# Self-attentions of a two-layer decoder: the product of the reciprocals at the head of TensorE's next turn, VectorE's normalisation behind the next tile's maxima and centred scores

## The chip, the core and the metric

The kernel runs on one core of a Trainium2 chip. The metric is the device time of one execution in microseconds. In the text PE is TensorE (PEld its weight loads), DVE is VectorE, ACT is ScalarE, POOL is GpSimd and SP is SyncE. L460 is line 460 of the kernel before.

## The reference, cut to what matters

`x` is (64, 64, 128) in float32: 64 sequences of 64 rows. Six blocks follow each other; the change is in the two self-attentions, which are the first block of each layer.

```python
x = x + L0_attn(layernorm(x))        # 16 heads of 8, biases, rotary embedding, causal
x = x + L0_xattn(layernorm(x), ctx, ctx, ...)
x = x + L0_ffn(layernorm(x), ...)
x = x + L1_attn(layernorm(x))        # 16 heads of 8, distance bias, causal
x = x + L1_xattn(ctx, layernorm(x), ...)
x = x + L1_ffn(layernorm(x), ...)

# inside an attention
scores = einsum('bhqd,bhkd->bhqk', q, k) / sqrt(8) + mask
attn = softmax(scores, axis=-1)
out = einsum('bhqk,bhkd->bhqd', attn, v).reshape(B, S, 128) @ wo
```

## The kernel before

The 4096 rows are cut into 32 tiles of 128 rows (two sequences each). `attention` is called for layer 0 (`rope` true) and layer 1. Each engine has a function `turn(t, u)`, unrolled over t, and in one turn it does different steps for different tiles: a software pipeline written out by hand. Engines meet through semaphores only, each engine runs its instructions in order, and `has(k)` leaves a step out where the tile does not exist.

For a tile k the steps are, with the DVE turn in which they stand:

- PE: projections to q and k (L439) and v (L450), some turns ahead. Scores (L475 adds mask and bias, L479 multiplies) into the banks `p_s`, in turn k - 2.
- DVE, turn k - 1: maxima of both halves of the heads (L499, L500), then the second half's centred scores (L504). ACT: exponentials of the first half (L613), of the second half (L630).
- DVE, turn k: sums (L510), reciprocals (L514), and their spreading over each head's 8 columns into `inv` (L516).
- PE, turn k: transposes of the probabilities (L418). At the end of the turn the product of `inv` and the identity (L460), which turns the reciprocals so that they fit the transposed output. It waits for `inverted` (L516) and for `oT_made` (L523 of the tile before, which still reads the same columns of `p_o`).
- PE, turn k + 1: probabilities times values (L407). ACT copies them out (L624). DVE, turn k + 1: L523 multiplies output and turned reciprocals to `oT`.
- PE, turn k + 2: output projection (L429). DVE, turn k + 2: adds the residual (L530, `x_made`), and takes the statistics for the next block's layernorm (L262, L267).
- POOL, turn k + 2: 1/sqrt of the variance (L281 and L283; in layer 1 L277, L279 and L283). DVE, at the very end of turn k + 2: the normalisation L290 (`norm.dve_norm`), which waits for POOL's L283.
- PE, turn k + 3: transpose of the normalised tile (L300), which waits for `x_made` of the following tile, as L530 reads the same bank `p_y`; ACT copies it out (L309, in layer 1 L306).
- POOL, in each turn and this order: in layer 0 the last step of the rotary embedding (L572, L575), the block-wise keys (L582, two operations; it waits for an earlier tile's scores to be done), in layer 0 the bias on the residual (L589), then the 1/sqrt operations.
- In layer 0 DVE also forms the terms of the rotary embedding (L542, four operations), which SP turns with a DMA; in layer 1 DVE copies q and k out (L552, L553). Both stand between the statistics and L290.

Of the kernel before, what the change touches and what calls it, by code (L numbers as in the profile page):

```python
# [22 lines left out]
P = 128  # L23
# [7 lines left out]
def has(k, n=NT):  # L31

    return not isinstance(k, int) or 0 <= k < n


def unrolled(eng, turn, first, last, ring):

    for t in range(first, last):
        turn(t, t % ring)
# [54 lines left out]
def col_bc(ap, n):  # L94

    p, m = ap.shape
    return ap.unsqueeze(2).to_broadcast([p, m, n])
# [233 lines left out]
def attention(nc, g, io, layer, at, later, later_loads):  # L331
# [3 lines left out]
    with Mem(nc, f"at{layer}") as m:  # L335
# [10 lines left out]
        inv, o_raw = m.sb("inv", [P, 2, NH, HD]), m.sb("o_raw", [P, P])  # L346
        pT = m.sb("pT", [P, 2, NH // 2, P])
        oT = m.sb("oT", [P, 2, P])
        p_qk, p_v, p_o, p_y = m.ps("p_qk"), m.ps("p_v"), m.ps("p_o"), m.ps("p_y")
# [7 lines left out]
        summed, inverted, inv_turned = m.sem("summed"), m.sem("inverted"), m.sem("inv_turned")  # L357
        o_copied, recip = m.sem("o_copied"), m.sem("recip")
        bv_spread, bv_done, bo_made = m.sem("bv_spread"), m.sem("bv_done"), m.sem("bo_made")
        pt_done, pt_copied, pv_done, oT_made, y_done = (m.sem(n) for n in ("pt_done", "pt_copied", "pv_done", "oT_made", "y_done"))  # L360
        x_part, x_made = m.sem("x_part"), m.sem("x_made")
        norm = Norm(m, g, x_made, twice=not rope)
# [22 lines left out]
        @block.tensor  # L385
        def _(pe):
            at["in"].wait(pe)
            if rope:
                pe.wait_ge(bv_spread, 1)
                pe.matmul(p_v[:, 0:D], bvb[:, :], w["wo"][:, :], start=True, stop=True).then_inc(bv_done, 1)  # L390
            wv = w["wv"][:, :].rearrange("i (j h d) -> i h j d", j=NH // 2, h=2)

            def turn(t, u):
                k, v = t - 1, (u - 1) % R
                if has(k):

                    pe.wait_ge(v_copied, 2 * (k + 1))
                    if has(k - 1):
                        pe.wait_ge(oT_made, k)
                    for c in range(4):  # L400
                        if c % 2 == 0:
                            pe.wait_ge(pt_copied, 2 * k + 1 + c // 2)
                        for b in range(PER):
                            for par in range(2):
                                j = 2 * c + par
                                at = 16 * (1 - par)
                                mm = pe.matmul(p_o[32 * c:32 * c + 32, b * S:(b + 1) * S], vblk[:, v, b, j, at:at + 32],  # L407
                                               pT[:, v % 2, j, b * S:(b + 1) * S], start=par == 0, stop=par == 1)
                    mm.then_inc(pv_done, 1)
                k, v = t, u  # L410
                if has(k):

                    for hf in range(2):
                        pe.wait_ge(c_exped if hf else exped, k + 1)
                        if has(k - 1):
                            pe.wait_ge(pt_copied, 2 * k + hf - 1)
                        for j in range(4):
                            mm = pe.transpose(p_t[hf][:, j * P:(j + 1) * P],  # L418
                                              pr[:, v, hf * half + j * P:hf * half + (j + 1) * P], g["ident"][:, :])
                        mm.then_inc(pt_done, 1)  # L420
                k = t - 2
                if has(k):

                    pe.wait_ge(oT_made, k + 1)
                    if has(k - 1):
                        pe.wait_ge(x_made, k)
                    if has(k - 2):
                        pe.wait_ge(norm.copied, k - 1)
                    pe.matmul(p_y[:, 0:D], oT[:, u % 2, :], w["wo"][:, :], start=True, stop=True).then_inc(y_done, 1)  # L429
                k = t + LEAD  # L430
                if has(k):

                    if has(k - 1):
                        if rope:
                            pe.wait_ge(rope_terms, 4 * k)
                        else:
                            pe.wait_ge(k_ready, k)
                    for i, n in enumerate(["wq", "wk"]):
                        mm = pe.matmul(p_qk[:, i * P:(i + 1) * P], w[n][:, :], g["xnT"][:, k * P:(k + 1) * P], start=True, stop=True)  # L439
                    mm.then_inc(qk_done, 1)  # L440
                k, v = t + 2, (u + 2) % R
                if has(k):

                    if has(k - 1):
                        pe.wait_ge(v_copied, 2 * k)
                    elif rope:
                        pe.wait_ge(bo_made, 1)
                    for h in range(2):
                        for b in range(PER):
                            mm = pe.matmul(p_v[S * h:S * h + S, b * S:(b + 1) * S], g["xnT"][:, k * P + b * S:k * P + (b + 1) * S],  # L450
                                           wv[:, h], start=True, stop=True)
                    mm.then_inc(v_done, 1)
                k, v = t, u
                if has(k):


                    pe.wait_ge(inverted, k + 1)
                    if has(k - 1):
                        pe.wait_ge(oT_made, k)
                    pe.matmul(p_o[:, P:2 * P], inv[:, v % 2, :, :].rearrange("p h d -> p (h d)"), g["ident"][:, :],  # L460
                              start=True, stop=True).then_inc(inv_turned, 1)
                k, v = t - 3, (u - 1) % 2
                if has(k):
                    if has(t - 2):
                        pe.wait_ge(x_made, t - 1)
                    norm.pe_transpose(pe, k, v, p_y[:, P:2 * P])
                k, v = t + 2, (u + 2) % R
                if has(k):

                    pe.wait_ge(q_ready, k + 1)  # L470
                    pe.wait_ge(kblk_ready, k + 1)
                    for hf in range(2):
                        if has(k - 1):
                            pe.wait_ge(centred if hf else exped, k)
                        pe.matmul(p_s[hf][:, :], pick[:, :], bias[:, hf * half:(hf + 1) * half], start=True, stop=False)  # L475
                    for b in range(PER):
                        for hf in range(2):
                            rows = slice(S * hf, S * hf + S)
                            mm = pe.matmul(p_s[hf][S * b:S * b + S, :], qT[rows, v, b * S:(b + 1) * S],  # L479
                                           kblk[rows, v % 2, b, :, :].rearrange("p h k -> p (h k)"), start=False, stop=True)  # L480
                    mm.then_inc(s_done, 1)

            unrolled(pe, turn, first, last, R)

        @block.vector
        def _(dve):
# [6 lines left out]
            def turn(t, u):  # L493
                k, v = t + 1, (u + 1) % R
                if has(k):

                    scores = [p_s[hf][:, :].rearrange("p (h k) -> p h k", h=HH) for hf in range(2)]
                    dve.wait_ge(s_done, k + 1)
                    dve.tensor_reduce(small[:, v, 0, 0:HH], scores[0], AX, ALU.max, negate=True).then_inc(maxed, 1)  # L499
                    dve.tensor_reduce(small[:, v, 0, HH:NH], scores[1], AX, ALU.max, negate=True).then_inc(maxed, 1)  # L500
                    if has(k - R):
                        dve.wait_ge(pt_done, 2 * (k - R + 1))
                    dve.wait_ge(maxed, 2 * k + 2)
                    dve.tensor_tensor(pr[:, v, half:].rearrange("p (h k) -> p h k", h=HH), scores[1],  # L504
                                      col_bc(small[:, v, 0, HH:NH], S), ALU.add).then_inc(centred, 1)
                k, v = t, u
                if has(k):

# [8 lines left out]
                k = t - 1  # L517
# [6 lines left out]
                k = t - 2  # L524
# [7 lines left out]
                k, v = t + LEAD, (t + LEAD) % 3  # L532
# [13 lines left out]
                k, v = t + 4, u  # L546
                if not rope and has(k):
# [3 lines left out]
                        dve.wait_ge(kblk_ready, k - R + 1)  # L551
                    dve.tensor_scalar(qT[:, v, :], p_qk[:, 0:P], float(HD) ** -0.5, None, ALU.mult).then_inc(q_ready, 1)  # L552
                    dve.tensor_copy(kT[:, v, :], p_qk[:, P:2 * P]).then_inc(k_ready, 1)  # L553
                if has(t - 2):
                    norm.dve_norm(dve, t - 2, u % 2)

            unrolled(dve, turn, first, last, R)

        @block.gpsimd
# [1593 lines left out]
```

## Time and profile before

| | us |
|---|---|
| median of 3 runs | 2044.24 (2042.54 to 2045.6) |
| the profiled execution, time | 2047.95 |
| the profiled execution, span | 2044.3 |
| self-attention of layer 0, stretch looked at | 57.0 to 255.2 |
| self-attention of layer 1, stretch looked at | 812.5 to 1017.0 |
| busy over the whole span: PE, DVE, ACT, POOL | 1860.7, 1466.0, 1435.5, 1126.0 |

Shares of the span are averages over stages with different limits, so the two stretches are to be read by themselves. In a row of the timeline the number in brackets is how long the engine stood idle before the instruction and what released it. Matmuls are pipelined and their ends are modelled.

### The profile page before, as it was taken

Reading aid. Unit: us, or ns where it says so; the run is one execution under the profiler, and the core shown is the slowest. Engines: PE = TensorE matmul, PEld = TensorE weight load, DVE = VectorE, ACT = ScalarE, POOL = GpSimd, SP = SyncE. Lnnn points to the kernel's source line nnn. Section 1 sums busy time; section 2 is a strip of 40 time slices with the busy share of each in tenths; the row PEclk is TensorE's granted clock in tenths of the full one; section 3 lists DMA queues with packets and bytes.
Section 4 is the critical chain, followed back from the end, with each engine's and each line's share of the span. In section 5 each row is a group of like instructions: output and inputs, shape, how many; then the busy total and the mean of one; then the engine's idle time right before and its main releaser. Section 6 shows DMA issues by size and latency. Waiting matters only on the chain. (4 is left out here: it accounts for less than half of the span.)

```text
span 2044.3 us, 62606 instructions
## 1 busy us (share of the span) xinstructions
PE 1860.7 (91%) x23443; PEld 1480.2 (72%) x23505; DVE 1466.0 (72%) x3927; ACT 1435.5 (70%) x4189; POOL 1126.0 (55%) x1453
## 2 busy tenths in 40 slices
PE   5899898699999998999799999768999999999998
PEld 3566566477777776666578888557888888888787
DVE  7799768666666665777656666578777777777567
ACT  5588767588888885888678888467666666666632
POOL 5677547588988898454423333157444444454420
PEclk9999999799999998999999999899999999999999
DMA  3011010232222222000011111200000000000101
GB/s 99 28 47 41 12 35 3 70 82 79 77 75 78 75 80 71 2 2 2 7 33 33 33 33 33 80 3 5 5 16 18 5 15 18 3 16 3 57 8 39
DMA packets 60620, 72.48 MB, mean 35 GB/s; under 512 B 10264, under 2 KB 38696, under 8 KB 60064
## 3 DMA queue, kind: packets, MB, share of 16 engines
q1 hardware_dynamic: 51104, 64.29, 10.9%
q10 hardware_dynamic: 9216, 4.20, 0.8%
q8 instruction: 188, 3.08, 0.6%
q14 instruction: 112, 0.92, 0.1%
HBM read 51.43 MB, written 4.44 MB: 27 GB/s over the span
## 5 line engine op out<-in xcount | busy, mean ns | idle before, releaser
L1094 POOL TENSOR_TENSOR ff_hl<-ff_hid,ff_hh 128x512 fp32r<-128x512 f32 x272 | 352.4, 1308 | 52.1 <-ACT ff_hh L1340 43.6
L1959 POOL TENSOR_TENSOR sm_zsum<-sm_zsum,sm_logits 128x512 f32<-128x512 f32 x120 | 154.7, 1289 | 271.2 <-ACT sm_logits L1985 269.5
L1262 DVE TENSOR_TENSOR ff_hid<-ff_p_b,ff_gates 128x512 f32<-128x512 f32 x240 | 163.7, 685 | 130.7 <-ACT ff_p_b L1329 130.7
L2002 ACT ACTIVATE sm_sT<-sm_p_s 128x512 f32<-128x512 f32 x128 | 69.5, 595 | 219.0 <-PE sm_p_s L1795 219.0
L613 ACT ACTIVATE at_pr<-at_p_s,at_small 128x64 f32<-128x64 f32 x512 | 154.8, 328 | 61.1 <-DVE at_small L499 61.1
L1340 ACT ACTIVATE ff_hh<-ff_hid 128x512 fp32r<-128x512 f32 x272 | 169.8, 624 | 17.8 <-DVE ff_hid L1262 16.7
L1329 ACT ACTIVATE ff_p_b<-ff_p_h,early_b 128x512 f32<-128x512 f32 x240 | 157.9, 658 | 33.1 <-PE ff_p_h L1151 28.7
L1971 POOL TENSOR_TENSOR sm_logits<-sm_logits,sm_peak 128x512 f32<-128x512 f32 x128 | 162.9, 1295 | 12.5 <-ACT sm_comb L2020 11.8
L1809 PE MATMUL sm_p_l<-g_phi,g_xnT 128*128 128x256 f32 x512 | 144.3, 409 | 26.2 <-ACT sm_logits L2030 25.1
L582 POOL TENSOR_TENSOR at_kblk<-at_kT,early_heads 128x512 f32<-128x512 f32 x128 | 131.7, 1049 | 29.5 <-PE at_p_s L479 27.3
L1908 DVE TENSOR_REDUCE sm_rmax<-sm_p_l 128x2 f32<-128x512 f32 x128 | 88.3, 690 | 63.3 <-PE sm_p_l L1809 62.7
L1843 PE MATMUL sm_p_y<-sm_w,sm_sT 128*32 128x128 f32 x4096 | 125.4, 274 | 9.1 <-ACT sm_combT L1992 8.4
L1809 PEld LDWEIGHTS sm_p_l<-g_phi,g_xnT 128*128 128x128 f32 x512 | 92.3, 199 | 55.0 <-ACT sm_logits L2030 27.7
L1851 PE MATMUL sm_p_o<-sm_yy,sm_combT 128*64 128x129 f32 x2048 | 127.4, 276 | 0.0
L1843 PE MATMUL sm_p_s<-sm_w,sm_sT 128*32 128x128 f32 x4096 | 124.9, 273 | 0.2
L1843 PEld LDWEIGHTS sm_p_y<-sm_w,sm_sT 128*32 128x32 f32 x4096 | 107.6, 110 | 22.7 <-ACT sm_sT L2002 11.6
L1940 DVE TENSOR_TENSOR sm_yy<-sm_p_y,sm_wb 128x512 f32<-128x512 f32 x128 | 88.0, 692 | 49.1 <-PE sm_p_y L1843 49.0
L1851 PEld LDWEIGHTS sm_p_o<-sm_yy,sm_combT 128*64 128x64 f32 x2048 | 110.3, 136 | 14.2 <-DVE sm_yy L1940 11.9
L1609 ACT ACTIVATE xa_pr<-xa_p_s,xa_sm 128x128 f32<-128x128 f32 x256 | 91.8, 391 | 39.0 <-DVE xa_sm L1521 39.0
L281 POOL TENSOR_TENSOR xa_n_rstd<-xa_n_mv,g_eps 128x1 f32<-128x1 f32 x32 | 20.6, 644 | 178.2 <-DVE xa_n_mv L267 178.2
L1149 PE MATMUL ff_p_h<-ff_xh,fw_w1h 128*128 128x512 f32 x272 | 113.2, 416 | 2.6 <-ACT ff_p_b L1329 2.2
L407 PEld LDWEIGHTS at_p_o<-at_pT,at_vblk 128*32 128x32 f32 x2048 | 78.9, 109 | 49.4 <-ACT at_vblk L640 48.7
(308 smaller groups left out, 5636.2 us busy)
## 6 DMA issues: line engine op xcount, KB each, us to landing
ff_gates<-kept_gates SPq DMA_DIRECT2D x120, 256.0 KB, 3.2
xa_kturn<-xa_ksin SPq DMA_DIRECT2D x128, 64.0 KB, 2.0
at_turned<-at_terms SPq DMA_DIRECT2D x64, 64.0 KB, 1.9
sm_w<-in_w_soft SPq DMA_DIRECT2D x8, 512.0 KB, 3.4
early_whole<-in_L_ffn_rW SPq DMA_DIRECT2D x30, 128.0 KB, 2.6
early_xs<-in_x ACTq DMA_DIRECT2D x32, 64.0 KB, 2.0
ld_ctx<-in_ctx ACTq DMA_DIRECT2D x32, 64.0 KB, 2.1
x_kept<-early_xs SPq DMA_DIRECT2D x1, 2048.0 KB, 7.4
```

What stands on the lines that cost most here:

```text
L582: op = pool.tensor_tensor(kblk[:, v % 2, b, :, :], row_bc(kT[:, v, b * S:(b + 1) * S], HH), col_bc(heads[:, :], S), ALU.mult)
L613: op = act.activation(pr[:, v, h * S:(h + 1) * S], p_s[0][:, h * S:(h + 1) * S], ACT.Exp, bias=small[:, v, 0, h:h + 1], accum_out=small[:, ...
L1094: eng.tensor_tensor(hl[:, q, :], hid[:, q, :], hh[:, q, :].bitcast(F32), ALU.subtract).then_inc(h_split, 1)
L1149: pe.matmul(p_h[n % PH][:, :], w1h[:, c, :], xh[:, u, :], start=True, stop=False)
L1262: dve.tensor_tensor(h, p_b[c % 2][:, :], gates[:, n % GR, :], ALU.mult).then_inc(scaled, 1)
L1329: act.activation(into, p_h[(NC_FF * t + c) % PH][:, :], ACT.Gelu, bias=b1[:, c:c + 1]).then_inc(gelud, 1)
L1340: act.activation(hh[:, q, :], hid[:, q, :], ACT.Copy).then_inc(h_rounded, 1)
L1809: mm = pe.matmul(p_l[h][:, a * CW:(a + 1) * CW], xnT[:, t * P:(t + 1) * P], phi[:, c % 2, :], start=True, stop=True)
L1843: mm = pe.matmul((p_y, p_s)[j % 2][a][SP * k:SP * (k + 1), (b * CQ + q) * D:(b * CQ + q + 1) * D], sT[:, j % 2, a, b, n_ * SP:(n_ + 1) * S ...
L1851: mm = pe.matmul(p_o[j % 2][b * S:(b + 1) * S, a * E1:a * E1 + D + 1], combT[:, j % RING_C, q, a, b * S:(b + 1) * S], yy[:, j % 2, a * PER ...
L1959: pool.tensor_tensor(z, z, logits[:, j % RING_L, :, :], ALU.add).then_inc(summed, 1)
L1971: pool.tensor_tensor(here, here, row_bc(peak[:, c % 2, :], TU), ALU.subtract).then_inc(centred, 1)
```

## The change

Two steps change places, in both self-attentions. On PE the product of the reciprocals of tile k, L460, goes from the end of turn k to the head of turn k + 1, ahead of the product of probabilities and values of the same tile. On DVE the normalisation L290 of tile k goes from the end of turn k + 2 into turn k + 3, behind the maxima and the centred scores and ahead of the sums.

```diff
@@ PE, turn
                     pe.wait_ge(v_copied, 2 * (k + 1))
                     if has(k - 1):
                         pe.wait_ge(oT_made, k)
+
+                    pe.wait_ge(inverted, k + 1)
+                    pe.matmul(p_o[:, P:2 * P], inv[:, v % 2, :, :].rearrange("p h d -> p (h d)"), g["ident"][:, :],
+                              start=True, stop=True).then_inc(inv_turned, 1)
                     for c in range(4):
...
                     mm.then_inc(v_done, 1)
-                k, v = t, u
-                if has(k):
-                    pe.wait_ge(inverted, k + 1)
-                    if has(k - 1):
-                        pe.wait_ge(oT_made, k)
-                    pe.matmul(p_o[:, P:2 * P], inv[:, v % 2, :, :].rearrange("p h d -> p (h d)"), g["ident"][:, :],
-                              start=True, stop=True).then_inc(inv_turned, 1)
                 k, v = t - 3, (u - 1) % 2
@@ DVE, turn
                     dve.tensor_tensor(pr[:, v, half:].rearrange("p (h k) -> p h k", h=HH), scores[1],
                                       col_bc(small[:, v, 0, HH:NH], S), ALU.add).then_inc(centred, 1)
+                if has(t - 3):
+                    norm.dve_norm(dve, t - 3, (u - 1) % 2)
                 k, v = t, u
...
                     dve.tensor_copy(kT[:, v, :], p_qk[:, P:2 * P]).then_inc(k_ready, 1)
-                if has(t - 2):
-                    norm.dve_norm(dve, t - 2, u % 2)
```

## Rows read from the trace of the kernel before

**Rows 1.** Busy time of the engines in the two stages, then clock and DMA.

```profile
core 0: us, PE busy (x) PEld busy (x) DVE busy (x) ACT busy (x) POOL busy (x), PEclk, DMA share, GB/s
57.00:255.20 198.20, 176.55 (x2105) 123.97 (x2135) 168.35 (x536) 153.86 (x737) 128.83 (x224) 0.99 0.11 32
812.50:1017.00 204.50, 178.59 (x2111) 126.20 (x2141) 148.18 (x480) 160.88 (x737) 97.87 (x163) 0.97 0.02 7
```

**Rows 2.** Timeline of a turn of layer 0: start, duration, engine, line.

```profile
120.87 0.69 DVE L499 TENSOR_REDUCE at_small<-at_p_s 128x8 f32<-128x512 f32 x1
...
122.87 0.68 DVE L510 TENSOR_REDUCE at_small<-at_pr 128x8 f32<-128x512 f32 x1
...
124.22 0.28 DVE L530 TENSOR_TENSOR early_xs<-at_p_y,early_xs 128x128 f32<-128x128 f32 x1
...
124.44 0.46 PE L460 MATMUL at_p_o<-g_ident,at_inv 128*128 128x128 f32 x2 [0.23 <-DVE at_oT L523]
...
124.63 0.14 PEld L300 LDWEIGHTS at_p_y<-g_ident,at_n_xn 128*128 128x128 f32 x1
...
124.96 0.18 DVE L267 BATCH_NORM_AGGREGATE at_n_mv<-at_n_stats 128x2 f32<-128x6 f32 x1
...
125.38 1.09 PE L479 MATMUL at_p_s<-at_kblk,at_qT 64*64 64x512 f32 x8
...
126.08 0.46 POOL L572 TENSOR_TENSOR at_qT<-at_terms,at_turned 128x128 f32<-128x128 f32 x1
...
126.22 0.40 DVE L290 TENSOR_SCALAR at_n_xn<-early_xs,at_n_mv,at_n_rstd 128x128 f32<-128x128 f32 x1
...
126.54 0.69 DVE L499 TENSOR_REDUCE at_small<-at_p_s 128x8 f32<-128x512 f32 x1
127.02 2.04 POOL L582 TENSOR_TENSOR at_kblk<-at_kT,early_heads 128x512 f32<-128x512 f32 x2
```

**Rows 3.** Timeline of a turn of layer 1.

```profile
900.51 0.68 DVE L499 TENSOR_REDUCE at_small<-at_p_s 128x8 f32<-128x512 f32 x1
...
903.84 0.28 DVE L530 TENSOR_TENSOR early_xs<-at_p_y,early_xs 128x128 f32<-128x128 f32 x1
...
905.00 1.09 PE L479 MATMUL at_p_s<-at_kblk,at_qT 64*64 64x512 f32 x8
...
906.11 0.35 DVE L290 TENSOR_SCALAR at_n_xn<-early_xs,at_n_mv,at_n_rstd 128x128 f32<-128x128 f32 x1 [0.90 <-POOL at_n_rstd L283]
906.27 2.09 POOL L582 TENSOR_TENSOR at_kblk<-at_kT,early_heads 128x512 f32<-128x512 f32 x2 [0.27 <-PE at_p_s L479]
906.37 0.68 DVE L499 TENSOR_REDUCE at_small<-at_p_s 128x8 f32<-128x512 f32 x1
```

**Rows 4.** Timeline of the drain of layer 0.

```profile
249.61 0.28 DVE L530 TENSOR_TENSOR early_xs<-at_p_y,early_xs 128x128 f32<-128x128 f32 x1
...
249.94 0.14 PEld L300 LDWEIGHTS at_p_y<-g_ident,at_n_xn 128*128 128x128 f32 x1 [0.66 <-DVE early_xs L530]
```

**Rows 5.** Timeline of turn 2 of layer 0 and the start of turn 3.

```profile
81.43 0.69 DVE L499 TENSOR_REDUCE at_small<-at_p_s 128x8 f32<-128x512 f32 x1 [1.09 <-PE at_p_s L479]
...
84.55 0.25 ACT L613 ACTIVATION_READ_ACCUMULATOR at_pr<-at_p_s,at_small 128x1 f32 x1
...
85.12 0.21 PEld L475 LDWEIGHTS at_p_s<-early_bias,early_pick 128*128 128x128 bf16 x2
...
85.36 0.18 DVE L267 BATCH_NORM_AGGREGATE at_n_mv<-at_n_stats 128x2 f32<-128x6 f32 x1
...
86.91 0.69 DVE L499 TENSOR_REDUCE at_small<-at_p_s 128x8 f32<-128x512 f32 x1
```

**Rows 6.** Instructions of L290 by tile: shortest, median, longest in ns.

```profile
L290 DVE TENSOR_SCALAR at_n_xn<-early_xs,at_n_mv,at_n_rstd x32: 345/398/400, 86.6 to 253.9; 128x128 f32<-128x128 f32 x32
...
L290 DVE TENSOR_SCALAR ff_n_xn<-early_xs,ff_n_mv,ff_n_rstd x32: 332/720/1287, 457.7 to 810.2; 128x128 f32<-128x128 f32 x32
```

**Rows 7.** Timeline of DVE and of POOL in the expert stage.

```profile
463.95 1.09 DVE L290 TENSOR_SCALAR ff_n_xn<-early_xs,ff_n_mv,ff_n_rstd 128x128 f32<-128x128 f32 x1
...
462.41 2.54 POOL L1094 TENSOR_TENSOR ff_hl<-ff_hid,ff_hh 128x512 fp32r<-128x512 f32 x2
```

## Prediction

> **What bounds the stages.** I read the busy times by stage first [rows 1]. The two self-attentions take 198.2 us and 204.5 us of the 2044.3 us span. No engine is full in either: PE is busy 176.55 and 178.59 us, DVE 168.35 and 148.18 us. What sets the pace is therefore a loop of waits between engines, which only the timeline of one turn shows. Below, T is the start of a turn's first maxima (L499) on DVE and times are counted from it.
>
> Layer 0 [rows 2]: T = 120.87, the next T is 126.54, so a turn takes 5.67 us. DVE reaches L530 at 3.35, right behind the multiplication L523. PE has its values (L450) out at 3.34 and then waits 0.23 us for L523 before the product L460 (3.57). The transpose L300 follows (weight load 3.76), then the scores L479 (4.51 to 5.60), and 0.07 us after their end the next L499 starts. The loop is DVE from L499 to L523, then PE from L460 to L479. DVE itself has almost no gap either.
>
> Layer 1 [rows 3]: T = 900.51, next 906.37, so 5.86 us. The scores end at 5.58, so PE would allow 5.65. But DVE stands 0.90 us before the normalisation L290, waiting for POOL's L283, and L499 is queued behind it. The loop is DVE up to its statistics, then POOL's three small operations, then L290 and L499.
>
> By the loop bounds there are 27 turns in each layer (t = 3 to 29) in which every part takes place.
>
> **L460 at the head of PE's turn.** No instruction is added. At its old place PE no longer waits for L523. L300, next in line, now meets its own wait bare: it wants L530 (`x_made`), because it writes the bank that L530 reads. L530 is the very next DVE instruction after L523. At the old place this wait was covered by L460: the load of L300 starts 0.19 us after the matmul of L460 and 0.13 us after the end of L530. Bare, the lag is 0.05 us (end 249.89, load 249.94, in the drain [rows 4]). From the load of L300 to the end of L479 it is 126.47 - 124.63 = 1.84 us, then 0.07 to L499. So PE's side would give: end of L530 (3.63) + 0.05 + 1.84 + 0.07 = 5.59 in layer 0, 5.56 in layer 1 (L530 ends at 3.61, L499 0.06 behind). The bound on the other side is the old lag of 0.13, giving 5.67 and 5.64. I take 0.05, since that row has the wait alone. The queue behind L300 is L475 and L479, and DVE waits for those.
>
> At its new place L460 puts about 0.2 us (124.44 to 124.63) before L407. Cover: PE's idle time before L300. The values end at about 3.54 instead of 3.34, and L530 ends at 3.63 at the earliest, later still once L290 is ahead of it. So it costs nothing; without cover it would be 0.2 us a turn. ACT's copies wait for nothing that moves beyond their own start.
>
> In turns 0 to 2 there is no L300, so L475 needs only the last ACT exponential. In turn 2 of layer 0 this ends at 84.80 and L475's load starts at 85.12 [rows 5]; less a 0.06 hand-over that is 0.26 us. Turns 0 and 1 have no L530 either and DVE's reciprocals and L523 are all that PE waits for; I take twice that for each. I put 1.3 us gained for layer 0 and 1.0 for layer 1, where rows 3 show the same PE timing (bounds 0 and 1.4 each).
>
> **L290 behind L504.** This takes L290 away from before L499 (in layer 1 the 0.90 us wait goes, as rstd is then a turn old) and puts it ahead of L510 to L530, which PE now waits for. Undisturbed it delays the next instruction by 0.26 (906.11 to 906.37). The cost on PE's loop is thus 0.26 a turn: layer 1 becomes 5.56 + 0.26 = 5.82 (bound above 5.90) against 5.86.
>
> In layer 0 something else is there. L290 takes 0.35 us in layer 1 [rows 3], 398 ns in the median of layer 0, and up to 1287 in the expert stage [rows 6]. One such case [rows 7]: L290 from 463.95 lasts 1.09, to 465.04, while POOL's two operations run from 462.41 to 464.95. L290 ends 0.09 after the POOL operation it met. In layer 0 the same: POOL's L572 runs 126.08 to 126.54 and L290 ends at 126.62. So L290 cannot finish while a POOL operation runs; it ends about 0.08 after it, and DVE's next starts 0.08 before L290's end, that is, with POOL's end.
>
> The new place of L290 is T + 2.00 (where L510 stands, 122.87). POOL's two L582 run there: 127.02 to 129.06, T + 0.48 to T + 2.52. L290 comes in the middle of the second. In layer 1 L582 starts 0.18 after the scores' end, T + 0.11, and lasts 2.04, to T + 2.15; 0.08 later is before L290's natural end (T + 2.33), so nothing is added there, with 0.10 to spare.
>
> In layer 0 L582's time hangs on DVE itself: L267 releases L281, then L283, L572, L575, L582. From L267 (124.96) to L582's end (129.06) is 4.10 us, without a gap. This closes a new loop: L510 to L267 is 2.09 (122.87 to 124.96), L267 to the end of L582 is 4.10, and L510 starts there behind L290. The turn becomes 6.19 us against 5.67. PE's loop then has slack: it needs 5.59 plus 0.26.
>
> The Trainium skill, "SBUF — State Buffer", section "SBUF: two separate sides", gives a rule for this: DVE's two-port modes and GpSimd share a port pair as an exclusive lock, and whichever starts first has it for the whole instruction. It speaks against the new place of L290; by the self-attentions' own largest excess (55 ns, 400 against 345) the layer 0 turn would be 5.90, by the rule 6.19. The trace agrees with the rule in the expert stage [rows 6, 7].
>
> **The sum.** Layer 0: start -1.3; turn 3 costs +0.7 (in turn 2 L267 is at 3.93, and the turn shrinks from 5.48 to 5.22 [rows 5], so L582 ends at 3.93 + 4.10 - 5.22 = 2.81 of turn 3, which takes 5.59 + 0.81 = 6.40); 26 turns x 0.52 = +13.5; L290 ahead of L510 in turn 30 +0.3; the drain keeps its order: 0. Together +13.2. Layer 1: -1.0; turn 3 5.82 against 5.65, +0.2; 26 x -0.04 = -1.0; turn 30 +0.3: -1.5 (bound above, 26 x 0.04 and 0.3 in turn 3: about +0.6). Total +11.7. The profiled execution took 2047.95 us, 3.7 over its span and 3.7 over the median 2044.24; it becomes 2059.7, and the median 2055.9.
>
> **Rivals.** Changes within 0.2% (4.1 us) count as no change, about what a measurement here can tell.
>
> *Forecast, the POOL operation holds L290 in layer 0:* 0.68. Own range 2052 to 2060. The low end is the loop 0.1 us shorter in its hand-overs and somewhat more gained at the start (-2.6 and -1); the high end is layer 1 at its upper bound and the start without a gain (+2.1 and +2.3).
>
> *L290 does not meet L582 that way, only its 0.26 counts:* 0.16. It would hold if the two slip past each other or operands matter. Layer 0 5.85, 27 x 0.18 = 4.9, -1.3, +0.3: +3.9; layer 1 -1.5; total +2.4, 2046.6. With the old 0.13 us lag 53 x 0.08 more: 2050.9. For it: layer 0 showed only 55 ns so far. Against: L290 was then at the tail of a 0.46 us operation. About 0.10 of this lies within 4.1 us.
>
> *Faster: L290 costs DVE nothing at its new place,* because it fills a gap between dependent operations: 0.10. Then the turns are 5.59 and 5.56: 27 x -0.08 - 1.3 and 26 x -0.30 - 0.1 - 1.0, total -12.4, 2031.8. For it: layer 1's wait for POOL is truly removed. Against: neither L504 nor L510 waits for the other's result, and L290 took 0.26 (layer 1) to 0.32 (layer 0) of DVE's time at its old place. It decides once L290's cost is under 0.16 us (8.3 / 53).
>
> *Worse: POOL's next operation (L589) goes before L290 as well:* 0.06. L589 is of the size of L572 (0.46 us), the turn about 6.63, 26 x 0.44 = 11.4 more: 2067. Against: the longest L290 in the expert stage, 1287 ns [rows 6], is about one POOL operation there (2.54 us for two, [rows 7]).
>
> **How the numbers follow.** Slower: 0.68 + 0.06 + 0.06 of the second case = 0.80; same 0.10; faster 0.10. The forecast's own range leaves out about 0.38; down to 2047 takes in most of the second case, and what is left out is the faster case, the worse one and a rest, about 0.2. Range 2047 to 2060.
>
> **What would show it.** L290 in layer 0 at 0.9 us or so, ending 0.08 behind L582; turns of 6.19 in layer 0 and about 5.82 in layer 1; PE idle before L300 with L530 as releaser, none before L460; in layer 1 no wait of L290 for L283 and a duration of 346 ns; turns 0 to 2 shorter. It is wrong if L290 in layer 0 stays near 400 ns, if layer 1's L582 reaches T + 2.25 and starts holding it too (each 0.1 us a turn is 2.6 us), or if the bare L300 is released later than 0.13.

## The result and the profile after

The changed kernel takes 2057.34 us (median of 5 runs, 2053.61 to 2059.16) against 2045.6 us for the kernel before, run beside it (5 runs). The ratio is 1.0054, with a 95% interval of 1.0043 to 1.0066. The forecast was 2055.9 us from a median of 2044.24, that is +11.7; measured is 2057.34 - 2045.6 = +11.7. The profiled execution has a span of 2057.0 us, 12.7 over that of before.

The kernel's lines moved by a few. In the changed kernel L494 and L495 are the maxima (L499, L500 before), L499 the centred scores (L504), L507 the sums (L510), L513 the spreading (L516), L527 the residual (L530), L576 the block-wise keys (L582), L566 and L569 the rotary step (L572, L575), L583 POOL's bias (L589), L402 the product (L460), L470 and L474 the bias and the scores (L475, L479). L290, L300 and L262 to L283 kept theirs. In the kernels of the experiments the numbers differ again by a few; the rows name what an instruction writes and reads.

The timeline of a turn of layer 0, which answers to [rows 2]; the turn's L494 stands at 120.90 (6.18 before the next):

```profile
121.52 2.04 POOL L576 TENSOR_TENSOR at_kblk<-at_kT,early_heads 128x512 f32<-128x512 f32 x2
...
122.90 0.74 DVE L290 TENSOR_SCALAR at_n_xn<-early_xs,at_n_mv,at_n_rstd 128x128 f32<-128x128 f32 x1
...
123.56 0.67 DVE L507 TENSOR_REDUCE at_small<-at_pr 128x8 f32<-128x512 f32 x1
...
124.90 0.28 DVE L527 TENSOR_TENSOR early_xs<-at_p_y,early_xs 128x128 f32<-128x128 f32 x1
...
125.23 0.14 PEld L300 LDWEIGHTS at_p_y<-g_ident,at_n_xn 128*128 128x128 f32 x1 [0.72 <-DVE early_xs L527]
...
125.65 0.18 DVE L267 BATCH_NORM_AGGREGATE at_n_mv<-at_n_stats 128x2 f32<-128x6 f32 x1
...
126.76 0.45 POOL L566 TENSOR_TENSOR at_qT<-at_terms,at_turned 128x128 f32<-128x128 f32 x1
...
127.08 0.69 DVE L494 TENSOR_REDUCE at_small<-at_p_s 128x8 f32<-128x512 f32 x1
...
127.70 2.04 POOL L576 TENSOR_TENSOR at_kblk<-at_kT,early_heads 128x512 f32<-128x512 f32 x2
...
129.75 0.67 DVE L507 TENSOR_REDUCE at_small<-at_pr 128x8 f32<-128x512 f32 x1
```

Read the first three rows together. POOL's two operations end at 123.56. L290 was started at 122.90, in the middle of the second, and ends at 123.64, 0.08 after it; L507 starts at 123.56. From there the loop can be added up: L507 to L267 is 2.09, L267 to the end of the next L576 (129.74) 4.09, and L507 follows 0.01 later: 6.19 us a turn. PE is not the bound any more: it stands before L300 with `early_xs L527` as releaser.

Layer 1, which answers to [rows 3]:

```profile
920.56 0.69 DVE L494 TENSOR_REDUCE at_small<-at_p_s 128x8 f32<-128x512 f32 x1 [0.82 <-PE at_p_s L474]
...
922.56 0.34 DVE L290 TENSOR_SCALAR at_n_xn<-early_xs,at_n_mv,at_n_rstd 128x128 f32<-128x128 f32 x1
...
924.16 0.28 DVE L527 TENSOR_TENSOR early_xs<-at_p_y,early_xs 128x128 f32<-128x128 f32 x1
...
924.49 0.14 PEld L300 LDWEIGHTS at_p_y<-g_ident,at_n_xn 128*128 128x128 f32 x1 [0.31 <-DVE early_xs L527]
924.56 0.20 PEld L470 LDWEIGHTS at_p_s<-early_bias,early_pick 128*128 128x128 bf16 x2
...
926.34 0.69 DVE L494 TENSOR_REDUCE at_small<-at_p_s 128x8 f32<-128x512 f32 x1 [0.82 <-PE at_p_s L474]
926.45 2.04 POOL L576 TENSOR_TENSOR at_kblk<-at_kT,early_heads 128x512 f32<-128x512 f32 x2
```

Here the wait of L290 for POOL's L283 is gone, and DVE waits for PE's scores instead. The turn is 5.78 us. L576 starts 0.11 after L494 and is over at T + 2.15. L290 starts at T + 2.00 and would end at T + 2.34 in any case, later than L576's end plus 0.08, so nothing is added to it.

The view of one line, L290, in layer 0 and in layer 1 of the changed kernel (shortest, median, longest in ns), against [rows 6]:

```profile
L290 DVE TENSOR_SCALAR at_n_xn<-early_xs,at_n_mv,at_n_rstd x32: 336/741/799, 86.0 to 264.9; 128x128 f32<-128x128 f32 x32
...
L290 DVE TENSOR_SCALAR at_n_xn<-early_xs,at_n_mv,at_n_rstd x32: 335/339/521, 858.5 to 1028.1; 128x128 f32<-128x128 f32 x32
```

**Where the 12.7 us of the profiled spans lie.** I take each self-attention from the maxima of turn 0 to those of turn 30. Layer 0: before 239.99 - 70.11 = 169.88, after 250.69 - 68.42 = 182.27, so +12.4. Layer 1: before 1000.56 - 825.48 = 175.08, after 1013.05 - 840.86 = 172.19, so -2.9. The ends of the two stages (to ACT's last copy) add 0.5 and 0.3. That is +10.3. The rest is not in code that changed. The two largest pieces are turn -1 of layer 0, 5.02 us instead of 6.34, and the stretch from the first matmul of the mLSTM stage (`L0_xattn` in the reference, the block behind layer 0's self-attention) to its first statistics: 30.07 us instead of 25.39 (+4.7). PE's mean granted clock over that stretch was 0.73 in the changed kernel's profile and 0.92 in that of before; that is, it stood at its lower level, 1.2 GHz, for longer. Two pieces of the stretch in the changed kernel's profile (the clock is the last column but two):

```profile
core 0: us, PE busy (x) PEld busy (x) DVE busy (x) ACT busy (x) POOL busy (x), PEclk, DMA share, GB/s
...
270.00:280.00 10.00, 8.32 (x55) 3.76 (x48) 4.34 (x16) 3.29 (x8) 0.00 (x0) 0.79 0.53 154
280.00:290.00 10.00, 9.66 (x75) 6.25 (x74) 2.51 (x10) 4.45 (x15) 0.00 (x0) 0.55 0.02 5
```

The first experiment shows that this comes and goes with the same kernel.

### The profile page after: what moved, and what is told of

It is laid out like the page before. It is cut to its first block and busy times, and to the rows that moved or that the text cites. A ratio compares the mean times of both kernels' runs of the same rounds, so it can differ in the third digit from the quotient of the medians.

```text
span 2057.0 us, 62544 instructions
## 1 busy us (share of the span) xinstructions
PE 1871.1 (91%) x23443; PEld 1483.6 (72%) x23505; DVE 1473.9 (72%) x3927; ACT 1435.5 (70%) x4189; POOL 1125.2 (55%) x1453
## 5 line engine op out<-in xcount | busy, mean ns | idle before, releaser
L1965 POOL TENSOR_TENSOR sm_logits<-sm_logits,sm_peak 128x512 f32<-128x512 f32 x128 | 163.4, 1298 | 12.7 <-ACT sm_comb L2014 12.1
L576 POOL TENSOR_TENSOR at_kblk<-at_kT,early_heads 128x512 f32<-128x512 f32 x128 | 130.7, 1042 | 22.4 <-PE at_p_s L474 17.0
L281 POOL TENSOR_TENSOR xa_n_rstd<-xa_n_mv,g_eps 128x1 f32<-128x1 f32 x32 | 20.6, 644 | 178.4 <-DVE xa_n_mv L267 178.4
L1837 PEld LDWEIGHTS sm_p_s<-sm_w,sm_sT 128*32 128x32 f32 x4096 | 113.7, 110 | 1.6 <-issue 1.5
```

The lines of the kernel that those rows point to most:

```text
L576: op = pool.tensor_tensor(kblk[:, v % 2, b, :, :], row_bc(kT[:, v, b * S:(b + 1) * S], HH), col_bc(heads[:, :], S), ALU.mult)
L1837: mm = pe.matmul((p_y, p_s)[j % 2][a][SP * k:SP * (k + 1), (b * CQ + q) * D:(b * CQ + q + 1) * D], sT[:, j % 2, a, b, n_ * SP:(n_ + 1) * S ...
L1965: pool.tensor_tensor(here, here, row_bc(peak[:, c % 2, :], TU), ALU.subtract).then_inc(centred, 1)
```

## The experiments

For every kernel the same two stretches (turn 0 to turn 30) and the usual turn were read from its profile; the ratios are those of the timed runs. The kernel before was timed again with each group of experiments: its median is 2047.25 us beside the first four and 2046.01 us beside the last four. In the table "both" is the sum of the two stretches less that of the kernel before.

| kernel | layer 0, turn | layer 0, 30 turns | layer 1, turn | layer 1, 30 turns | both | time against before |
|---|---|---|---|---|---|---|
| before | 5.66 | 169.88 | 5.86 | 175.08 | | |
| the change | 6.19 | 182.27 | 5.78 | 172.19 | +9.5 | 1.0054 (1.0043 to 1.0066) |
| `again` | 6.19 | 182.48 | 5.78 | 172.27 | +9.8 | 1.005 (1.0035 to 1.0064) |
| `pe_only` | 5.65 | 168.39 | 6.67 | 193.07 | +16.5 | 1.0089 (1.0069 to 1.011) |
| `dve_only` | 6.19 | 183.66 | 5.92 | 176.46 | +15.2 | 1.0051 (1.0034 to 1.0069) |
| `layer1_only` | 5.66 | 169.86 | 5.78 | 172.26 | -2.8 | 0.998 (0.9968 to 0.9992) |
| `pool_order` | 5.87 | 174.72 | 5.78 | 172.27 | +2.0 | 1.0015 (0.9998 to 1.0033) |
| `quarters` | 5.90 | 175.45 | 5.96 | 176.63 | +7.1 | one run, 2058.3 us |
| `norm_late` | 5.53 | 165.77 | 5.53 | 164.83 | -14.4 | 0.9913 (0.9893 to 0.9932) |
| `norm_late_pool` | 5.80 | 170.90 | 5.53 | 164.83 | -9.2 | one run, 2039.68 us |

**The changed kernel once more** (no edit).

> The changed kernel once more, unchanged. Turns of 6.19 us in layer 0 and 5.78 in layer 1 should be there again. What is open is the beginning of the mLSTM stage: in the profile of the changed kernel PE's granted clock was at its lower level there and the stage's first statistics came 4.7 us later than before. If that is chance, it is missing in some executions (4 to 5 us shorter then); if the change causes it, it is there each time. Ratio to before 1.003 to 1.007.

2057.39 us (4 runs) against 2047.25. Both layers' turns are those of the first profile. The mLSTM stretch took 296.16 - 270.50 = 25.66 us this time, against 30.07 in the first profile. The low clock was over sooner, and the mean over the stretch was 0.91 in place of 0.73:

```profile
270.00:280.00 10.00, 8.92 (x56) 3.68 (x56) 6.13 (x19) 3.48 (x7) 0.36 (x1) 0.74 0.46 126
280.00:290.00 10.00, 8.21 (x118) 5.80 (x118) 2.80 (x11) 7.06 (x24) 0.00 (x0) 1.00 0.14 41
```

But turn -1 was back at 6.34 us. So either may happen to the same kernel. Over the two groups (nine runs of the changed kernel) the medians differ from those of before by 11.7 and 10.1 us all the same.

**PE's part alone.** The diff of the change without its DVE lines:

```diff
-                if has(t - 3):
-                    norm.dve_norm(dve, t - 3, (u - 1) % 2)
...
+                if has(t - 2):
+                    norm.dve_norm(dve, t - 2, u % 2)
```

> Only PE's part: the product at the head of the next turn, the normalisation at its old place. Theory A (the normalisation at DVE's end and POOL's operations set layer 0's turn as well, since it ends with POOL's L572): layer 0 stays at 5.67 us a turn, layer 1 at 5.86, only turns 0 to 2 get shorter, about -2 us in all. Theory B (PE's wait for L523 was what bound layer 0): layer 0 goes to 5.55, about -5 us.

2063.62 us against 2047.25, where theory A had forecast 2 us less than before: slower than the whole change. Layer 0 stays at 5.65 us as theory A had it. But layer 1, which both theories left at 5.86, went to 6.67. Its timeline shows why:

```profile
924.24 1.14 DVE L290 TENSOR_SCALAR at_n_xn<-early_xs,at_n_mv,at_n_rstd 128x128 f32<-128x128 f32 x1 [0.91 <-POOL at_n_rstd L283]
924.26 2.05 POOL L577 TENSOR_TENSOR at_kblk<-at_kT,early_heads 128x512 f32<-128x512 f32 x2
...
925.31 0.68 DVE L494 TENSOR_REDUCE at_small<-at_p_s 128x8 f32<-128x512 f32 x1
```

Before the change L290 started at 906.11 and POOL's keys at 906.27, as they were waiting for PE's scores [rows 3]; L290 was in first and took 0.35 us. PE's part brings the scores forward, from 5.58 to 5.44 us after T, so the keys no longer wait for them: they follow right behind L283, the same POOL instruction that releases L290. POOL's keys (L577 here) now start 0.02 us after L290, POOL gets ahead of it, and L290 is held to the end of the first of the two, 1.14 us. L494 is behind it. The view of the line says the same for 26 of the layer's 32 tiles (median 1146 ns):

```profile
L290 DVE TENSOR_SCALAR at_n_xn<-early_xs,at_n_mv,at_n_rstd x26: 345/1146/1150, 839.9 to 1004.2; 128x128 f32<-128x128 f32 x26
```

The row of L577 is two operations in 2.05 us, back to back, and L290 ends at 925.38, about 0.08 after the first of them. It got its turn between the two, so the hold lasts for one operation and not until POOL stands idle.

**DVE's part alone.** L290 behind the centred scores, L460 at its old place. Against the kernel before:

```diff
+                if has(t - 3):
+                    norm.dve_norm(dve, t - 3, (u - 1) % 2)
...
-                if has(t - 2):
-                    norm.dve_norm(dve, t - 2, u % 2)
```

> Only DVE's part: the normalisation behind the centred scores, the product at its old place. Theory A (the POOL operation holds the normalisation, and L510, L267 and POOL form a loop): layer 0 6.19 us a turn as with both parts, layer 1 about 5.9 (PE's old loop of 5.65 plus 0.26): +14 to +16 us. Theory B (only the normalisation's own 0.26 counts, behind PE's loop): layer 0 5.93, layer 1 5.9: +9 us.

2056.28 us against 2047.25. Both turns are those of theory A: 6.19 and 5.92. So the loss in layer 0 comes from DVE's part alone. By the stretches the kernel lost 15.2 us, by the medians 9. Most of the difference goes with PE's granted clock, which over the whole execution was higher in these runs (0.973 to 0.981, mean 0.9785) than in those of before (0.973 to 0.978, mean 0.9756). At equal clock, one run at each of two clocks, the loss is that of the stretches: the run at 0.973 took 2064.09 us, where the three of before at 0.973 average 2049.3 (+14.8), and the run at 0.978 took 2059.89, where the four of before at 0.978 average 2044.9 (+15.0). That the change itself raised the clock is not shown.

**Both parts, in layer 1 alone.**

```diff
+                if not rope and has(t - 3):
+                    norm.dve_norm(dve, t - 3, (u - 1) % 2)
...
-                if has(t - 2):
+                if rope and has(t - 2):
                     norm.dve_norm(dve, t - 2, u % 2)
```

(against the kernel before, and in the same way at PE's two places)

> Both parts, in layer 1 alone. Theory A: all of the loss comes from layer 0, so this is 2 to 3 us faster than before (layer 1 at 5.78 us a turn against 5.86 and a shorter start). Theory B (layer 1 gives nothing that lasts, its gain is lost behind it): no difference.

2042.43 us (10 runs) against 2047.25, ratio 0.998 (0.9968 to 0.9992): theory A. The stretches give -2.8 us, the medians -4.8; the 2 us between them are no more than the scatter of single runs. Layer 1's gain lasts; all of the loss is layer 0's.

**POOL's order changed in layer 0, on top of the change.**

```diff
                 k, v = t + 3, (u + 3) % R
-                if rope and has(k):
-                    pool.wait_ge(rope_turned[k % 2], 32 * (k // 2 + 1))
...
+                k, v = t + 4, u
+                if rope and has(k):
+                    pool.wait_ge(rope_turned[k % 2], 32 * (k // 2 + 1))
...
```

The removed lines stood ahead of the keys; the added ones stand behind the bias and ahead of the 1/sqrt.

> The changed kernel, and in layer 0 POOL's last rotary step (q and k of a tile, old L572 and L575) goes from ahead of the block-wise keys (old L582) to behind the residual's bias, for one tile further ahead. The keys then no longer hang on DVE's L267 through four operations; they start when the scores are done, T + 0.11, and end at T + 2.15, before the normalisation at T + 2.00 needs the port. Theory A (a running POOL operation holds the normalisation): layer 0 goes from 6.19 to 5.8 to 5.9 us a turn, the normalisation back to 0.35 us, about 8 us faster than the change. Theory B (the place in DVE's order costs it, whatever POOL does): 6.19 as before.

2050.15 us (10 runs) against 2046.01; layer 0 5.87 us a turn, theory A. Over the 30 turns layer 0 is 7.6 us shorter than in the change, where about 8 were forecast. The medians show less, +4.1 us against before where the change had +10.1 and +11.7, and by its interval (0.9998 to 1.0033) this kernel can't be told from the kernel before. DVE's order was not touched, so it is what POOL does at that time that cost the change 0.3 us a turn. The timeline:

```profile
121.30 2.04 POOL L567 TENSOR_TENSOR at_kblk<-at_kT,early_heads 128x512 f32<-128x512 f32 x2 [0.40 <-PE at_p_s L474]
...
123.19 0.34 DVE L290 TENSOR_SCALAR at_n_xn<-early_xs,at_n_mv,at_n_rstd 128x128 f32<-128x128 f32 x1
123.30 0.54 POOL L574 TENSOR_TENSOR early_xs<-early_xs,early_bo 128x128 f32<-128x128 f32 x1
...
124.22 0.45 POOL L584 TENSOR_TENSOR at_kT<-at_terms,at_turned 128x128 f32<-128x128 f32 x1
124.44 0.32 DVE L513 COPY at_inv<-at_small 128x128 f32<-128x128 f32 x1
```

L290 is back at 0.34. Two smaller signs: POOL's L574 takes 0.54 instead of 0.45, as L290 was in first; and L513, the copy that spreads the reciprocals, takes 0.32 instead of 0.23, as it meets POOL's L584 and ends 0.09 behind it.

**The keys in four operations in place of two, on top of the change.**

```diff
                     for b in range(PER):
-                        op = pool.tensor_tensor(kblk[:, v % 2, b, :, :],
+                        for q in range(2):
+                            hq = slice(q * HH // 2, (q + 1) * HH // 2)
+                            op = pool.tensor_tensor(kblk[:, v % 2, b, hq, :],
...
```

> The changed kernel with the block-wise keys made in four operations of half the size in place of two. Theory A, with the hold lasting to the end of the one operation that is running: operations of about 0.55 us; the normalisation is held to the end of the third, about 0.5 us long, and the layer 0 turn is 2.09 + 2.06 + 3 x 0.55 = 5.8 us. Theory C (it is held until POOL stands idle or the whole block is done): 6.2 us or more.

Layer 0 5.90 us a turn and L290 0.46, close to theory A (5.8 and 0.5) and away from theory C:

```profile
126.84 2.33 POOL L578 TENSOR_TENSOR at_kblk<-at_kT,early_heads 128x256 f32<-128x256 f32 x4
128.22 0.46 DVE L290 TENSOR_SCALAR at_n_xn<-early_xs,at_n_mv,at_n_rstd 128x128 f32<-128x128 f32 x1
128.60 0.67 DVE L507 TENSOR_REDUCE at_small<-at_pr 128x8 f32<-128x512 f32 x1
```

Four operations take 2.33 us, so the third ends at about 126.84 + 3 x 0.58 = 128.58, and L290 at 128.68. L290 was released while the fourth was still to run. The miss of 0.1 us is the operation's size (0.58, not 0.55). In layer 1 the longer block now reaches L290 (515 ns in the median) and costs 0.18 us a turn. The kernel's one run, 2058.3 us, is no shorter than the change: the two stretches give back only 2.4 us, and its mLSTM stretch took 30.1 us at a mean granted clock of 0.73, as in the first profile of the change.

**The normalisation late.** L460 as in the change. L290 behind L267 of the same turn, where nothing on the way to L530 waits for it; PE's transpose L300 and ACT's copy for tile t - 4 instead of t - 3, L429's wait for that copy one tile earlier, and one turn more at the end:

```diff
-                        pe.wait_ge(norm.copied, k - 1)
...
+                        pe.wait_ge(norm.copied, k - 2)
...
-                k, v = t - 3, (u - 1) % 2
+                k, v = t - 4, u % 2
...
                     norm.dve_stats(dve, k, u % 2)
+                if has(t - 3):
+                    norm.dve_norm(dve, t - 3, (u - 1) % 2)
...
```

> The product of the reciprocals as in the change; the normalisation behind the statistics of the next tile (behind L267, off the way to L530), and PE's transpose of it and ACT's copy one turn later, with one turn more at the end. Theory A (turns are set by L510 to L530, PE's scores and the port): layer 0 about 5.6 us a turn (DVE's own sum is 5.61), layer 1 5.52 (5.78 less 0.26), about 12 us faster than before, less some 2 us for the turn at the end. Theory B (PE or ACT is full by then, or the later transpose comes back as a wait): layer 1 at 5.7 or more, no gain over the kernel before.

2029.31 us against 2046.01, ratio 0.9913 (0.9893 to 0.9932): faster than both kernels. It gained more than was forecast: 14.4 us in the two stretches and 16.7 by the medians, against about 10. Layer 1 came out as forecast (5.53 for 5.52), layer 0 0.07 us a turn better (5.53 for 5.6), and the turn more at the end cost nothing: from the last maxima to ACT's last copy the layers take 14.45 and 15.08 us, against 14.93 and 16.10 before. The layer 1 turn is 0.25 under the change's, as much as L290 was expected to cost ahead of L510 (0.26).

```profile
127.03 0.14 PEld L300 LDWEIGHTS at_p_y<-g_ident,at_n_xn 128*128 128x128 f32 x1
...
127.54 0.35 DVE L290 TENSOR_SCALAR at_n_xn<-early_xs,at_n_mv,at_n_rstd 128x128 f32<-128x128 f32 x1
...
127.76 0.19 POOL L281 TENSOR_TENSOR at_n_rstd<-at_n_mv,g_eps 128x1 f32<-128x1 f32 x1 [1.34 <-DVE at_n_mv L267]
...
128.88 0.69 DVE L494 TENSOR_REDUCE at_small<-at_p_s 128x8 f32<-128x512 f32 x1
```

L290 starts 0.22 us ahead of L281, for which POOL had stood idle, so it is in first and is not held (346 and 347 ns in the median of the two layers).

**Both, the late normalisation and POOL's new order.**

> Both: the late normalisation and POOL's new order. Theory A: in layer 0 POOL's two rotary operations now run at T + 2.6 to 3.5, where DVE spreads the reciprocals (L516 at T + 3.0, the other DVE instruction that a POOL operation can hold). L516 gets 0.1 to 0.5 us longer and the layer 0 turn 5.7 to 5.9, worse than with the late normalisation alone. If only the normalisation can be held: 5.6 as there.

2039.68 us, one run. Layer 0 at 5.80 us, 0.27 worse than with the late normalisation alone, as theory A had it. Here L290 is not held (346 ns), but L511, the spreading copy, is (500 ns in the median of layer 0, against 226 with the late normalisation alone):

```profile
129.42 0.45 POOL L584 TENSOR_TENSOR at_kT<-at_terms,at_turned 128x128 f32<-128x128 f32 x1
129.43 0.53 DVE L511 COPY at_inv<-at_small 128x128 f32<-128x128 f32 x1
129.88 0.28 DVE L518 TENSOR_TENSOR at_oT<-at_p_o,at_o_raw 128x128 f32<-128x128 f32 x1
```

The same order of POOL that took 7.6 us from the change's layer 0 adds 5.1 us here, since what counts is which of DVE's two such instructions it meets.

## Why the prediction was right

**The hold in layer 0.** Right, in mechanism and in size: 6.19 us a turn was forecast and measured. `pool_order` and `quarters` show that it is the running POOL operation and not the place in DVE's order, `dve_only` that PE's part has nothing to do with it. The list of signs said 0.9 us for L290; by the text's own terms (end of L582 at T + 2.60, plus 0.08, less 2.00) it should have said 0.7, and 0.74 was measured. The hold also ends one turn sooner than I counted: the last L582 stands in turn 28, and turn 29 took 5.78.

One sentence of the prediction is too wide, "L290 cannot finish while a POOL operation runs". In its own rows 3 L290 runs from 906.11 to 906.46, although POOL's L582 runs from 906.27 on. It is held only by an operation that was in first. With that condition the ten profiles agree: each of the 242 L290 of the self-attentions that lasted over 365 ns ends 0.08 to 0.09 us behind the end of a POOL operation, and in all 217 cases where a POOL operation was under way when L290 started and still had over 0.29 us to run, L290 was held.

**The sum.** Layer 0 was forecast at +13.2, of which the 30 turns have +12.4 and its end +0.5. Its start came out at -1.2 (forecast -1.3) although its parts did not: turn 2 fell only from 5.48 to 5.38 (5.22 forecast), and turns 0 and 1 together gained 1.1 (1.0 forecast). Turn 3 took 6.11 and not 6.40 us, and turns 4 to 29 gave +13.1 for +13.5. Layer 1 was forecast at -1.5; the turns have -2.9 and the end +0.3. Its start gave 0.7 and not 1.0, its turns 4 to 29 gave 2.4 and not 1.0. Of these 2.4, 0.4 are turn 28 alone, which had taken 6.21 us before. The usual turn came out at 5.78 and not 5.82: after a bare wait L300's successor starts its weight load 0.07 us behind that of L300, where I had taken over 0.11 from the covered case. Together +10.3, against +11.7 forecast. That the medians hit +11.7 to a tenth is luck: the second set of runs has +10.1, and single runs of the kernel before lie between 2038.98 and 2052.14 us.

**What bound layer 0 before.** Half right. I named DVE up to L523 and PE from L460 to L479. `pe_only` takes that wait away and the turn stays at 5.65. There was a second loop of the same length: L499 to L267 4.09 us, L267 to the end of L572 1.58, and L290, held by L572, lets L499 go exactly then: 5.67. The rows were all there [rows 2], and I used them only for the duration of L290. This second loop is hardly longer than DVE's own work in its order: the hold makes L290 400 ns instead of 346, so without it the turn would be about 5.6 us by my estimate.

**L460 costs nothing at its new place.** True for the change as a whole, but for a reason that I had not seen in full. In layer 1 PE's part alone costs 0.81 us a turn, since scores that end sooner start POOL's keys sooner, so close behind L290's start that POOL is in first. The change escapes this because it takes L290 away from there.

**The rivals.** "L290 does not meet L582", "L290 costs nothing" (5.78 us a turn with it ahead of L510 in layer 1, 5.53 without) and "L589 goes first as well" (`quarters`: L290 comes in between two POOL operations) are all excluded.

The clock in the mLSTM stage was in none of the cases. Of the ten profiles, the first of the changed kernel and that of `quarters` have the stretch at 30.1 us and a mean granted clock of 0.73; in the eight others, `again` among them, it took 24.6 to 25.9 us. Whether the change makes it likelier is open; so few profiles don't tell.

## What to carry to other kernels

Where DVE and POOL work side by side, look for a DVE instruction whose duration varies for one and the same shape. Here the normalisation and the spreading copy were held by the POOL operation that was running, up to its end, and everything behind them in DVE's order was held too. Place such an instruction where POOL is waiting, and check again after every change that moves POOL's work in time, on PE too. A move off a wait pays only if the slot where it lands isn't on the next longest loop: the same two steps gave 1.0054 with the normalisation ahead of the sums and 0.9913 with it behind the statistics and PE's transpose of it a turn later.

## What was not expected of the hardware

A seventh of a microsecond decided between 0.35 and 1.14 us. With POOL's operation starting 0.16 after L290, DVE was first; with 0.02 after it, POOL was. With no other POOL operation under way, none of the ten profiles has one that starts between 0.03 and 0.15 us after an L290, so nothing here narrows it down further. L290 does not take what it shares with POOL at the start that the timeline shows. Nor does POOL, as far as one row tells: in `pool_order` L290 ended at 123.53, 0.23 us after the start of L574, which lost only 0.09 us by it.

The Trainium skill, "SBUF — State Buffer", section "SBUF: two separate sides", says that whichever of the two starts first has the shared ports for the whole instruction. The holds here agree (L290 and the spreading copy end 0.08 to 0.09 us after POOL's operation, POOL's own bias took 0.54 instead of 0.45 us when L290 was first), with the one refinement that the start in the timeline is not the moment that counts.
